# A two-layer expert kernel: the first tiles centred by a plain sum, one power for both halves ahead of GpSimd's last ctx piece, no filler matmul between the first transposes

## The reference

```
def _layernorm(x, eps=1e-05):
    return (x - mean(x)) / sqrt(var(x) + eps)

# layer 1: 4 experts, the expert of a token is read off its id
e   = min(clip(id, 0, 12499) // 3125, 3)
z   = n(x) @ ctx[e].T                # ctx serves as gate, up and down
x   = x + (silu(z) * z) @ ctx[e].T

# layer 2: router over 16 experts, the best 4 are weighted, and one shared expert
s   = sigmoid(n(x) @ router.T);  top 4 of s + bias;  weights s / sum(s)
x   = x + sum_e w_e * (silu(n(x) @ g_e.T) * (n(x) @ u_e.T)) @ d_e.T + shared(n(x))
```

## Time and profile before

| | us |
|---|---|
| median of the three runs | 169.66 |
| the profiled execution's own time | 169.34 |
| its span, first to last instruction | 167.2 |
| around the span | 2.1 |
| PE busy | 162.5 (97%) |
| DVE busy | 114.5 (68%) |
| ACT busy | 68.7 (41%) |
| POOL busy | 37.2 (22%) |

### The profile page before, as it was taken

The page is one execution under the profiler, slowest core; times in us unless marked ns, Lnnn a source line. Parts: engine busy times, 40 slices in busy tenths (PEclk is TensorE's granted clock), DMA queues, the critical chain, the costliest instruction groups (busy, mean ns, idle before and its releaser), DMA issues.

```text
span 167.2 us, 2186 instructions
## 1 busy us (share of the span) xinstructions
PE 162.5 (97%) x705; PEld 128.9 (77%) x705; DVE 114.5 (68%) x237; ACT 68.7 (41%) x116; POOL 37.2 (22%) x36
## 2 busy tenths in 40 slices
PE   7999999999999999999999999999999999999992
PEld 2788888888778888888888878888888888888880
DVE  1889999666957998779986744967714444444462
ACT  3654342831359134536734538452222222222210
POOL 1384000656241045556970000000000000000000
PEclk9999999999999999999999999999999999999999
DMA  5891380164304065987225400025441112200003
GB/s 172 275 408 44 107 291 0 21 206 161 115 4 127 16 205 192 219 240 211 67 61 163 153 0 4 1 103 165 173 141 67 63 63 63 65 0 0 4 0 125
DMA packets 12199, 18.78 MB, mean 112 GB/s; under 512 B 3772, under 2 KB 6044, under 8 KB 12060
## 3 DMA queue, kind: packets, MB, share of 16 engines
q1 hardware_dynamic: 12188, 18.64, 34.9%
HBM read 16.39 MB, written 2.24 MB: 111 GB/s over the span
## 4 chain that ended last, share of the span: by engine, by line
PE 95%; DMA 2%; DVE 1%; DVEq 0%; issue 0%
PE bank L1030 23%; PE bank L1131 15%; PE bank L1129 13%; PE bank L1130 13%; PE bank L1149 7%; PE bank L1152 7%; PE bank L1150 7%; DMA first<-first_d 2%; PE bank L998 1%; PE bank L1071 1%; PE bank L1065 1%; PE bank L1126 1%; PE bank L1125 1%; PE bank L987 1%; PE bank L1078 1%; PE bank L1060 1%
## 5 line engine op out<-in xcount | busy, mean ns | idle before, releaser
L1131 PE MATMUL bank<-xn_lo,gu_hi 128*128 128x512 f32 (+1 forms) x104 | 41.1, 395 | 0.0
L1129 PE MATMUL bank<-xn_hi,gu_lo 128*128 128x512 f32 x96 | 38.0, 396 | 0.0
L1130 PE MATMUL bank<-xn_hi,gu_hi 128*128 128x512 f32 x96 | 38.0, 396 | 0.0
L599 ACT ACTIVATE h_hi<-hid 128x512 fp32r<-128x512 f32 (+1 forms) x26 | 16.4, 632 | 45.6 <-DVE hid L860 45.6
L865 DVE TENSOR_TENSOR h_lo<-hid,h_hi 128x512 fp32r<-128x512 f32 (+1 forms) x26 | 18.0, 691 | 14.9 <-ACT h_hi L599 14.9
L1131 PEld LDWEIGHTS bank<-xn_lo,gu_hi 128*128 128x128 f32 (+1 forms) x104 | 19.4, 187 | 4.9
L589 ACT ACTIVATE act_sb<-bank 128x512 f32<-128x512 f32 (+1 forms) x26 | 15.4, 592 | 17.5 <-PE bank L1131 17.4
L472 POOL TENSOR_TENSOR gu_lo<-stage,gu_hi 128x512 fp32r<-128x512 f32 x12 | 17.2, 1457 | 21.7 <-ACT gu_hi L504 16.3
L1129 PEld LDWEIGHTS bank<-xn_hi,gu_lo 128*128 128x128 f32 x96 | 18.0, 188 | 4.4
L1130 PEld LDWEIGHTS bank<-xn_hi,gu_hi 128*128 128x128 f32 x96 | 18.0, 188 | 4.3
L749 DVE COPY_PREDICATED prod<-beyond,bank 128x512 f32<-128x512 uint8 x24 | 17.6, 737 | 5.1 <-PE bank L1030 4.4
(11 more groups left out here) (102 smaller groups left out, 213.2 us busy)
## 6 DMA issues: line engine op xcount, KB each, us to landing
stage<-gu_d SPq DMA_DIRECT2D x6, 512.0 KB, 3.9
stage<-wd_d SPq DMA_DIRECT2D x3, 512.0 KB, 4.3
first<-comb_d SPq DMA_DIRECT2D x8, 192.0 KB, 2.9
ids<-comb_d SPq DMA_DIRECT2D x8, 192.0 KB, 3.3
stage<-ctx_d SPq DMA_DIRECT2D x4, 256.0 KB, 6.0
xt<-xt_d SPq DMA_DIRECT2D x1, 1024.0 KB, 9.9
first<-comb_d SPq DMA_DIRECT2D x8, 128.0 KB, 3.0
ids<-comb_d SPq DMA_DIRECT2D x8, 128.0 KB, 2.9
```

Source lines behind the costliest of these rows:

```text
L1129: nc.tensor.matmul(out[:], gu_lo[:, cols], xn_hi[:, h, k], start=(k == 0), stop=False)
L1130: nc.tensor.matmul(out[:], gu_hi[:, cols], xn_hi[:, h, k], start=False, stop=False)
L1131: ins = nc.tensor.matmul(out[0:rows, :], gu_hi[:, wide], xn_lo[:, h, k], start=False, stop=(k == KC - 1))
```

## The change

Four things are done. DVE's `centre` replaces three instructions (statistics, aggregate, subtract with a scalar) by two: a sum over the 256 features into `minus_mean`, and one scalar-tensor-tensor that multiplies the sum, broadcast over 256 columns, by -1/256 and adds `x`. Since `centre` then leaves no statistics behind, DVE computes those of all four tiles of half 0 later, in place of two. One 256-column filler matmul between the second and third tile's transposes goes. POOL raises the variances of both halves to the power -0.5 in one instruction of 8 columns (in place of two of 4), into `deviation`; it stands ahead of the subtraction of ctx piece 3, where the two powers stood behind it, and waits until DVE has written the variances of both halves. Readers of the powers of half 1 take them from `deviation`.

```diff
-        power = sb("power", [P, TT])
+        power = sb("power", [P, HALVES * TT])
...
+        def inverse_deviation(n):
+            return deviation[:, n * TT:(n + 1) * TT] if n < HALVES else rstd[:, n]
...
+            def first_deviations():
+
+                pool.wait_ge(varied, HALVES)
+                nc.gpsimd.tensor_tensor(deviation[:, 0:HALVES * TT], vareps[:, 0:HALVES].rearrange("p n t -> p (n t)"),
+                                        power[:], ALU.pow).then_inc(powered, HALVES)
...
-            for n in range(E1):
+            for n in range(E1 - 1):
                 low_part(n)
-            rstd_of(0)
-            rstd_of(1)
+            first_deviations()
+            low_part(E1 - 1)
...
             def centre(t):
                 dve.wait_ge(x_in[t // (TT // 2)], 16)
-                tile_stats(0, t)
+                step(nc.vector.tensor_reduce(minus_mean[:, t:t + 1], x[:, t], AX.X, ALU.add))
                 dve.wait_ge(dstep, steps[0])
-                step(nc.vector.bn_aggr(meanvar[:, 0, t], stats[:, t]))
-                dve.wait_ge(dstep, steps[0])
-                nc.vector.tensor_scalar(xn[:, t], x[:, t], meanvar[:, 0, t, 0:1], None, ALU.subtract).then_inc(normed_v, 1)
+                nc.vector.scalar_tensor_tensor(out=xn[:, t], in0=minus_mean[:, t:t + 1].to_broadcast([P, D]), scalar=-1.0 / D, in1=x[:, t],
+                                               op0=ALU.mult, op1=ALU.add).then_inc(normed_v, 1)
...
-            tile_stats(0, 1)
-            tile_stats(0, 3)
-            layer_norm_vars(0, (1, 3))
+            for t in range(TT):
+                tile_stats(0, t)
+            layer_norm_vars(0)
...
-                for t, warm_steps in enumerate((0, 0, 1, 0)):
-                    keep_warm(warm_steps, HALF // 2)
+                for t in range(TT):
                     wait_normed(pe, 0, t)
```

More of the change, by code:

```diff
@@ L473, in low_part @@
                 ins.then_inc(w_lo, 1)
+            def first_deviations():
+                pool.wait_ge(varied, HALVES)
+                nc.gpsimd.tensor_tensor(deviation[:, 0:HALVES * TT], vareps[:, 0:HALVES].rearrange("p n t -> p (n t)"),
+                                        power[:], ALU.pow).then_inc(powered, HALVES)
             def rstd_of(n):
                 pool.wait_ge(varied, n + 1)
-                nc.gpsimd.tensor_tensor(deviation[:, 0:TT] if n == 0 else rstd[:, n], vareps[:, n], power[:], ALU.pow).then_inc(powered, 1)
+                nc.gpsimd.tensor_tensor(rstd[:, n], vareps[:, n], power[:, 0:TT], ALU.pow).then_inc(powered, 1)
             nc.gpsimd.memset(comb[:], 0.0).then_inc(comb_zero, 1)
@@ L542, in apply_norm @@
                         nc.scalar.activation(xn[:, t], tile_to_norm(n, t), ACT.Identity, bias=shift[:, n, t:t + 1],
-                                             scale=rstd[:, n, t:t + 1]).then_inc(normed_a, 1)
+                                             scale=inverse_deviation(n)[:, t:t + 1]).then_inc(normed_a, 1)
             def hidden_high(b):
@@ L712, in layer_norm_apply @@
                 dve.wait_ge(powered, n + 1)
-                nc.vector.scalar_tensor_tensor(out=shift[:, n], in0=meanvar[:, n, :, 0], scalar=-1.0, in1=rstd[:, n],
+                nc.vector.scalar_tensor_tensor(out=shift[:, n], in0=meanvar[:, n, :, 0], scalar=-1.0, in1=inverse_deviation(n),
                                                op0=ALU.mult, op1=ALU.mult).then_inc(shifted, 1)
@@ L720, in layer_norm_apply @@
                     if t in BY_VECTOR[n]:
-                        nc.vector.tensor_scalar(xn[:, t], tile_to_norm(n, t), meanvar[:, n, t, 0:1], rstd[:, n, t:t + 1],
+                        nc.vector.tensor_scalar(xn[:, t], tile_to_norm(n, t), meanvar[:, n, t, 0:1], inverse_deviation(n)[:, t:t + 1],
                                                 ALU.subtract, ALU.mult).then_inc(normed_v, 1)
```

## The result

The changed kernel takes 170.33 us (median of six runs, 169.78 to 170.56), the kernel before 169.45 in the same set: a ratio of 1.0044, with an interval of 1.0027 to 1.0061, or 0.75 us slower (0.46 to 1.03); the two medians themselves lie 0.88 apart. One execution of those reported further down, of the kernel that writes both variances with one instruction, took 231.87 us at a granted clock of 0.66 and is in no ratio. The profiled execution took 170.56 us with a span of 168.4, 1.2 more than before.

What follows compares the result with a forecast made beforehand. PE, which waits only twice, was taken to bound the kernel. `shift` ending at 15.89 instead of 14.75 is 1.14 us late; less 0.26 slack, 0.88 slower: 170.5 us against the median 169.66, range 169.5 to 171.4.

Steps and rivals of the forecast that it cites:

- Step 1, centring: DVE's first tiles: two instructions of 0.42 and 0.43 us replace three; the first tile is ready 0.16 us earlier.
- Step 2, the filler and the cap by `ctx_lo`: PE's start: transposes end 0.31 us earlier, but waiting for POOL's ctx_lo piece 0 caps the gain at 0.25 us.
- Step 3 (a), the held variances: DVE's variances of half 0, issued at 10.09, held by a POOL piece to about 11.34; half 1's statistics 0.67 us late.
- Step 3 (b), the power: POOL's one power of 8 columns ahead of half 1's `shift`: taken as 1.2 us, between 1.03 and 2.06.
- Step 3 (c), piece 3 holding `shift`: POOL's ctx piece 3 runs where DVE issues `shift`, which ends 1.27 us after the power's end, not 1.02.
- The wait: PE's transposes of half 1: a new wait for ACT's normalised tile of 0.9 to 1.1 us.
- slack: ACT's last tile of half 1 was usable 0.26 to 0.27 us before PE reached its transposes.
- The terms costed at nothing: Later reload of `rstd_all`, DVE's work behind it, and h of half 0, needed only in the fourth mix: no cost.
- the variances get in between the pieces: Half 0's variances on DVE are not held by POOL: net 0.21 us slower, 169.9 us; chance 0.2.
- the power costs by the column: POOL's power of 8 columns takes near 2.06 us: 171.4 us with variances held; chance 0.2.
- POOL and DVE don't meet: Variances not held and `shift` passes beside piece 3: net -0.21 to -0.04 us, 169.45 to 169.6 us; chance 0.1.
- The late clock: PE's rise to 2.4 GHz comes 3.7 us later without the filler: net 1.6 us slower, 171.3 us; chance 0.05.

Runs made afterwards that it cites:

- GpSimd's part undone: Changed kernel with two powers of 4 columns again, behind ctx piece 3; plain sum and missing filler stay: 169.41 against 169.38 us, ratio 1.0006.
- the experiment that isolates it: Changed kernel with two powers of 4 columns in place of one of 8, still ahead of ctx piece 3: 169.79 against 169.40 us, ratio 1.0023.
- GpSimd's part alone: Kernel before with only the one power of 8 columns put ahead of ctx piece 3: 170.07 against 169.38 us, ratio 1.0036.
- padded: Kernel before with an unused tile of 32 bytes a partition behind the tile of powers: 165.44 against 169.49 us, ratio 0.9765.
- half 1 first: Changed kernel with two powers behind ctx piece 3, half 1's first, and half 1's shift and normalising ahead on DVE: 169.37 against 169.40 us, ratio 0.9998.

## Why the prediction was right, and where its sizes were off

The direction and the size came out (0.88 forecast; 0.75 by the ratio, 0.88 between the medians; 170.33 is inside the range), and so did the mechanism: two parts that save at the start, a chain from the load over half 1's `shift` that ends later, and a new wait of PE for half 1's tiles. By its steps:

- Step 1, centring: 0.42 and 0.43 forecast, 0.42 and 0.42 measured. The first transpose stands 1.02 behind the start of centring (4.95 - 3.93); before it was 5.03 - 3.85 = 1.18. The saving is 0.16 as forecast.
- Step 2, the filler and the cap by `ctx_lo`: the matmuls on it were forecast 0.25 earlier and came 0.19 earlier behind a load 0.08 later. Right, as far as this goes; but that the sum and the filler would be worth 0.25 "left alone" is not borne out by any median. The cap is not POOL's work only, it is the load of ctx piece 0, and that varies (it lands between 5.1 and 6.4 us over the profiles).
- Step 3 (a), the held variances: right in mechanism and instant (10.12 against 10.09), not the cost of 0.67 in this profile. Here POOL's pieces themselves ran late (9.31 instead of 8.79), so that the hold ended at 10.64, where even the load of before (10.65) would have hidden it. In the profile with GpSimd's part undone it cost 0.6: the load had landed at 10.75 and the statistics started at 11.36. The term belongs to some executions; I had made it a part of every one.
- Step 3 (b), the power: 1.2 forecast, 1.68 measured. This is the mis-sized term, 0.48 too low. I took the row of 4 columns as the nearest; the runs show a fixed part of 0.4 and 0.16 for each column.
- Step 3 (c), piece 3 holding `shift`: 0.25 forecast, 0.48 - 0.16 = 0.32 measured, and 0.76 - 0.16 = 0.60 in the experiment that isolates it, where `shift` was issued earlier into the piece.
- The wait: forecast at ACT's tile, 0.9 to 1.1. The row of the profile has 1.1, at the first transpose and for DVE's tile, but ACT's tile ends the chain as forecast. `shift` and ACT's tile came 1.52 later than before; less a slack of 0.30 (forecast 0.26) that is 1.22, and PE's mix went on 17.64 - 16.43 = 1.21 later. The terms costed at nothing were nothing: behind that matmul both kernels take 150.8 us.

With (a) at nothing and (b) at 1.68 the sum is 12.75 + 1.68 + 1.27 - 14.75 - 0.26 = 0.69. The central value owed its nearness to two errors of opposite sign, 0.67 too much in (a) and 0.48 too little in (b), and so to luck in part. Of the rivals, "the variances get in between the pieces" had the better sum, with a power longer than it assumed, though not for its reason: the variances were held (0.52 in place of 0.17), only not past the load; "the power costs by the column" was mostly right (1.68 of a possible 2.06). "POOL and DVE don't meet" fell with every `shift` beside a piece (0.48, 0.49, 0.76). The late clock by 3.7 us didn't happen in any profile: the matmuls of 256 columns run at 0.12 spacing from the second on in the changed kernel too (eight in 1.34 us). Nor is its 5.7 us from PE's first matmul to the rise a fixed time here, as the last section shows.

## What to carry to other kernels

Where an engine never waits, as PE here, a gain ahead of it lasts only up to the next thing that hangs on a transfer: find that chain and its slack before pricing the gain. A wait row can name the first tile that an engine lacked and not the one that held it longest, as with GpSimd's part alone; compare the instants behind the whole group. A four-column instruction on DVE can last as long as a GpSimd piece if it is issued beside one (1.31 us in place of 0.17), so small instructions on a chain should not stand where the other engine has just begun. And two kernels that differ in a tile's size may differ in where all later tiles start; check that before a difference is given to the order of the work.

## What the runs showed of the hardware that was not expected

- Matmuls of 512 columns of 4-byte data start every 0.227 us when the tile that they read starts at a multiple of 64 bytes in its partition, every 0.233 when it starts 32 past one. Over this kernel that is 4.0 us of 169.5. The starts are worked out from tile sizes, and that the moving operand is what matters, not another of the tiles that move along (`prod`, `act_sb`, `hid`), is inferred: the matmuls gained alike whichever of these tiles they read (`xn_hi`, `xn_lo`, `h_hi`, `h_lo`: 0.232 to 0.234 us before, 0.226 to 0.228 padded), and the weight tiles did not move. It was not tested one by one.
- A power on GpSimd costs 0.16 us for a column of 128 rows and 0.4 fixed (1.03, 1.68, 2.95 for 4, 8, 16 columns; 4 columns took 1.01 to 1.19 over the profiles, but 1.38 or 1.39 in the last norm, which nothing here explains).
- TensorE's rise from 1.2 to 2.4 GHz moves from execution to execution though PE did the same before it: in the profile with half 1 first eight transposes took 1.46 us, in the changed kernel's 1.94, both behind the same zeros. It is read from the spacing of starts, 0.21 us for a transpose ahead of it and 0.11 behind, since the granted clock of the profile reads full on both sides of it. It fell between 5.3 and 6.9 us of the span in the five profiles with the filler, between 4.4 and 7.1 in the nine without: no effect of the filler can be seen.
- The load of tiles 4 to 7, issued at the same time in all kernels (3.53 or 3.54 us), landed anywhere from 9.6 to 11.4 us.
